# Wide attention layer of a twelve-layer kernel: where GpSimd computes its roots and sine products, and how the last output projection is portioned

## The reference

```python
# layer 10: 16 query heads of 128, 4 key/value heads, 2048 context rows + 128 own rows, batch of 2
q = rms_norm((x @ wq).reshape(B, L, 16, 128), q_norm_w)
k = rms_norm((x @ wk).reshape(B, L, 4, 128), k_norm_w)
v = (x @ wv).reshape(B, L, 4, 128)
k_ctx = rms_norm((h_ctx_kv @ wk_ctx).reshape(B, T, 4, 128), k_norm_w)
v_ctx = (h_ctx_kv @ wv_ctx).reshape(B, T, 4, 128)
q = q * cos + rotate_half(q) * sin
k = k * cos + rotate_half(k) * sin
...
scores = jnp.einsum('blhd,bmhd->bhlm', q, k_full) * scale + mask     # causal on the own rows
out = jnp.einsum('bhlm,bmhd->blhd', softmax(scores), v_full)
x = x + out.reshape(B, L, 16 * 128) @ wo
...
# layer 12: weights and activations rounded to float8 (e4m3) before each product
x = x + qdot(gelu(qdot(h, w_gating[0])) * qdot(h, w_gating[1]), w_linear)
```

## Time and profile before

| what | value |
|---|---|
| three timed runs | 1133.62, 1134.43 (median), 1134.64 us |
| the profiled execution, its own time | 1135.64 us |
| its span on the core | 1133.7 us |
| mean granted clock of TensorE | 0.975 |
| front of the wide layer, TensorE's first projection to its first score | 621.55 to 648.07 us |
| loop with 32 units | 648.07 to 1063.9 us |

### The profile page before, as it was taken

The page is one execution under the profiler, slowest core; times in us unless marked ns, Lnnn a source line. Parts: engine busy times, 40 slices in busy tenths (PEclk is TensorE's granted clock), DMA queues, the critical chain, the costliest instruction groups (busy, mean ns, idle before and its releaser), DMA issues.

```text
span 1133.7 us, 23178 instructions
## 1 busy us (share of the span) xinstructions
PE 1037.2 (91%) x9488; PEld 846.4 (75%) x9488; DVE 698.7 (62%) x1333; ACT 504.3 (44%) x871; POOL 234.0 (21%) x356
## 2 busy tenths in 40 slices
PE   6989999989999879999987989999999999999785
PEld 3755778866666545776775778999999999989664
DVE  3755243257777358888744776776666566677366
ACT  3242221126666437888855634433423223322374
POOL 5601048302122000000010511210010233331120
PEclk9998999998999979999999999999999999999897
DMA  9611346545663516000141000131111221100000
GB/s 387 274 74 63 137 159 222 195 120 141 175 172 100 173 39 235 22 3 2 38 150 38 1 1 20 38 113 38 38 57 38 60 63 57 57 20 10 0 2 10
DMA packets 37156, 100.37 MB, mean 89 GB/s; under 512 B 4032, under 2 KB 12608, under 8 KB 35392
## 3 DMA queue, kind: packets, MB, share of 16 engines
q1 hardware_dynamic: 33152, 87.35, 23.5%
q0 software_dynamic: 2752, 9.44, 2.5%
q10 hardware_dynamic: 1152, 2.16, 0.5%
HBM read 83.73 MB, written 15.20 MB: 87 GB/s over the span
## 4 chain that ended last, share of the span: by engine, by line
PE 71%; DVE 16%; issue 4%; POOL 4%; ACT 4%; DMA 1%; DVEq 0%; SPq 0%; ACTq 0%; POOLq 0%
PE ps L2192 9%; PE ps L390 8%; PE ps L2149 6%; PE ps L1372 6%; PE ps L1723 5%; PE ps L446 3%; PE ps L1714 3%; PE ps L383 3%; PE ps L2047 3%; PE ps L1520 3%; PE ps L2036 2%; DVE prob L2343 2%; PE ps L1058 2%; PE ps L1050 2%; DVE st L1649 2%
## 5 line engine op out<-in xcount | busy, mean ns | idle before, releaser
L2192 PE MATMUL ps<-vv,prob 128*128 128x129 f32 x1024 | 128.2, 278 | 2.6 <-DVE xn L2379 2.6
L2192 PEld LDWEIGHTS ps<-vv,prob 128*128 128x128 f32 x1024 | 121.7, 194 | 3.3 <-ACT prob L2298 3.0
L1649 DVE TENSOR_REDUCE st<-ps 128x1 f32<-128x512 f32 x128 | 83.4, 687 | 26.6 <-PE ps L1520 21.2
L2331 DVE TENSOR_REDUCE probT<-ps 128x128 f32<-128x1024 f32 x64 | 82.5, 1288 | 19.8 <-PE ps L2149 12.9
L2298 ACT ACTIVATE prob<-prob 128x1024 f32<-128x1024 f32 x64 | 71.1, 1111 | 27.4 <-DVE prob L2343 27.4
L390 PE MATMUL ps<-xT,big 128*128 128x256 f32 x352 | 79.8, 381 | 0.8 <-ACT xT L673 0.7
L2271 ACT COPY w<-ps 128x128 f32<-128x128 f32 x32 | 8.5, 265 | 161.7 <-PE ps L2158 161.7
L2343 DVE TENSOR_TENSOR prob<-ps,probT 128x1024 f32<-128x1024 f32 x64 | 79.6, 1286 | 1.1
L1596 ACT ACTIVATE prob<-ps 128x1024 f32<-128x1024 f32 x64 | 65.7, 1029 | 29.3 <-PE ps L1531 27.9
L152 POOL TENSOR_SCALAR small<-small 128x4 f32<-128x4 f32 (+1 forms) x44 | 13.0, 296 | 304.4 <-DVE small L2086 154.1
L390 PEld LDWEIGHTS ps<-xT,big 128*128 128x128 f32 x352 | 66.2, 190 | 11.3 <-ACT xT L673 0.9
(11 more groups left out here) (461 smaller groups left out, 2266.9 us busy)
## 6 DMA issues: line engine op xcount, KB each, us to landing
big<-blocks_in SPq DMA_DIRECT2D x22, 768.0 KB, 4.5
big<-ctxT_in SPq DMA_DIRECT2D x24, 512.0 KB, 4.1
key_parts<-w POOLq DMA_DIRECT2D x16, 384.0 KB, 5.3
kt<-key_parts SPq DMA_DIRECT2D x32, 192.0 KB, 3.3
vv<-ctx_in SPq DMA_DIRECT2D x2, 2176.0 KB, 23.9
vv<-early_values SPq DMA_DIRECT2D x4, 1088.0 KB, 12.8
kt<-ctxT_in SPq DMA_DIRECT2D x2, 2048.0 KB, 11.6
kt<-key_parts SPq DMA_DIRECT2D x32, 128.0 KB, 3.3
```

The source lines that it names most:

```text
L1649: dve.tensor_reduce(self.mx[:, u % 2, n:n + 1], k.ps[:, n % 2, :], AX.X, ALU.max).then_inc(s("reduced"), 1)
L2192: last = pe.matmul(k.ps[:, 7, 0:DH + 1], self.prob(u)[:, ch * P:ch * P + P], v, start=(ch == 0), stop=(ch == MC))
L2331: dve.tensor_reduce(self.largest[:, h * P:(h + 1) * P], bank.rearrange("p (c t) -> p t c", t=P), AX.X, ALU.max).then_inc(s("c3_max"), 1)
```

## The change

Three edits and one swap.

1. **Loop.** In steps 18 to 26 GpSimd's list was: add, subtract, root of the step's key group, load. It is now: add, root, subtract, load. (`weights_gpsimd` is cut into `weights_raised` and `weights_rounded`.)
2. **Front.** For q0 to q3 of batch 0 the product with the sines leaves VectorE's list; GpSimd makes it into another buffer (`sines`, `by_sine`). One semaphore, `w_own_made`, now counts roots and sine products in GpSimd's order (`SINES`, `SCALES`). The memsets `ones` come later. On ScalarE, `scale_heads` of q3 now precedes `square` of key group 4.
3. **End.** The output projection's heads in steps 28 to 32 were 4, 4, 3, 2, 1 and are now 3, 3, 3, 4, 1.

```diff
-    LAST_HEADS = {28: range(0, 4), 29: range(4, 8), 30: range(8, 11), 31: range(11, 13), 32: range(13, 14)}
+    LAST_HEADS = {28: range(0, 3), 29: range(3, 6), 30: range(6, 9), 31: range(9, 13), 32: range(13, 14)}
...
         o.step(dve.tensor_tensor(t3, h3, bc(self.table[:, first], 1, 4), ALU.mult))
-        o.step(dve.tensor_tensor(h3, h3, bc(self.table[:, first + 1], 1, 4), ALU.mult))
+        if b == 0 and n:
+            dve.wait_ge(s("w_own_made"), self.SINES[n])
+            h4 = self.by_sine(n).rearrange("p h (a d) -> p h a d", a=2)
+        else:
+            o.step(dve.tensor_tensor(h3, h3, bc(self.table[:, first + 1], 1, 4), ALU.mult))
...
+    def sines(self, pool, n):
+        k, s = self.k, self.k.s
+        pool.wait_ge(s("w_heads"), self.MADE.index(self.ROPED[n]) + 1)
+        if n >= 3:
+            pool.wait_ge(s("w_rope"), n - 1)
+        pool.tensor_tensor(self.by_sine(n), self.heads[0][n].rearrange("p (h d) -> p h d", h=4), bc(self.table[:, 1], 1, 4),
+                           ALU.mult).then_inc(s("w_own_made"), 1)
...
         self.copy_turned(act, 0, 2, 2)
+        self.scale_heads(act, 0, 4)
         self.square(act, 4, 3)
-        self.scale_heads(act, 0, 4)
...
         self.own_scales(pool, o, 0)
+        self.sines(pool, 1)
+        self.sines(pool, 2)
+        self.query_scales(pool, o, 0, 1)
+        self.sines(pool, 3)
+        self.query_scales(pool, o, 0, 2)
+        self.sines(pool, 4)
+        self.query_scales(pool, o, 0, 3)
         self.ones(pool, o)
-        for n in (1, 2, 3):
-            self.query_scales(pool, o, 0, n)
...
             if u >= self.EIGHT_AT:
-                eight.weights_gpsimd(pool, o, dram, u - self.EIGHT_AT)
+                eight.weights_raised(pool, o, u - self.EIGHT_AT)
             self.scales(pool, o, g)
             if u >= self.EIGHT_AT:
-                eight.weights_load(pool, dram, u - self.EIGHT_AT + 2)
+                eight.weights_rounded(pool, dram, u - self.EIGHT_AT)
```

More of the change, by code:

```diff
@@ L1861 @@
     EIGHT_AT = 18
-    LAST_HEADS = {28: range(0, 4), 29: range(4, 8), 30: range(8, 11), 31: range(11, 13), 32: range(13, 14)}
+    LAST_HEADS = {28: range(0, 3), 29: range(3, 6), 30: range(6, 9), 31: range(9, 13), 32: range(13, 14)}
     FIRST_VALUES = (0, 4, 1, 5, 2, 3)
     KEY_BANKS = (6, 7, 4, 5, 3)
+    SINES = (0, 2, 3, 5, 7)
+    SCALES = ((1, 4, 6, 8, 9), (10, 11, 12, 13, 14))
     def __init__(self, k):
@@ L1981, in rope @@
             o.step(last)
-            dve.wait_ge(s("w_own_rs"), 5 * b + 1)
+            dve.wait_ge(s("w_own_made"), self.SCALES[b][0])
             last = dve.tensor_tensor(t3, t3, bc(self.rs_k[b], 2, DH), ALU.mult)
@@ L1988, in scale_heads @@
         act.wait_ge(k.s("w_rope"), 5 * b + n + 1)
-        act.wait_ge(k.s("w_own_rs"), 5 * b + n + 1)
+        act.wait_ge(k.s("w_own_made"), self.SCALES[b][n])
         for h in range(4):
@@ L2019, in ones, with by_sine @@
         o.step(pool.memset(self.vs[:, :, :, DH:DH + 1], 1.0))
+    def sines(self, pool, n):
[5 more added lines that the diff above has]
+                           ALU.mult).then_inc(s("w_own_made"), 1)
+    def by_sine(self, n):
+        return self.heads[1][n].rearrange("p (h d) -> p h d", h=4)
     def own_scales(self, pool, o, b):
@@ L2023, in own_scales @@
         pool.wait_ge(s("w_own_ssq"), 5 * b + 1)
-        rsqrt_pool(k, pool, o, self.rs_k[b], self.ssq_k, 1.0 / DH, 1e-6, 4).then_inc(s("w_own_rs"), 1)
+        rsqrt_pool(k, pool, o, self.rs_k[b], self.ssq_k, 1.0 / DH, 1e-6, 4).then_inc(s("w_own_made"), 1)
     def query_scales(self, pool, o, b, n):
@@ L2412, in gpsimd @@
             if u >= self.EIGHT_AT:
-                eight.weights_gpsimd(pool, o, dram, u - self.EIGHT_AT)
+                eight.weights_raised(pool, o, u - self.EIGHT_AT)
             self.scales(pool, o, g)
             if u >= self.EIGHT_AT:
-                eight.weights_load(pool, dram, u - self.EIGHT_AT + 2)
+                eight.weights_rounded(pool, dram, u - self.EIGHT_AT)
         for i in range(self.GROUPS - F - self.EIGHT_AT, eight.PIECES):
-            eight.weights_gpsimd(pool, o, dram, i)
-            eight.weights_load(pool, dram, i + 2)
+            eight.weights_raised(pool, o, i)
+            eight.weights_rounded(pool, dram, i)
 class Differential:
@@ L2612, in weights_load, with weights_raised, weights_rounded @@
         pool.dma_start(self.raw[i % 2], dram["w8"][:, 512 * i:512 * i + 512]).then_inc(s(f"e8_in{i % 2}"), 16)
-    def weights_gpsimd(self, pool, o, dram, i):
-        s = self.k.s
+    def weights_raised(self, pool, o, i):
+        raw, tmp = self.raw[i % 2], self.tmp[i % 2]
+        pool.wait_ge(self.k.s("e8_power"), i + 1)
+        o.step(pool.tensor_tensor(raw, raw, tmp, ALU.add))
+    def weights_rounded(self, pool, dram, i):
         raw, tmp = self.raw[i % 2], self.tmp[i % 2]
         to = self.w_up[:, 512 * i:512 * i + 512] if i < 8 else self.w_down[:, 512 * i - 4096:512 * i - 3584]
-        pool.wait_ge(s("e8_power"), i + 1)
-        o.step(pool.tensor_tensor(raw, raw, tmp, ALU.add))
-        pool.tensor_tensor(to, raw, tmp, ALU.subtract).then_inc(s("e8_w"), 1)
+        pool.tensor_tensor(to, raw, tmp, ALU.subtract).then_inc(self.k.s("e8_w"), 1)
+        self.weights_load(pool, dram, i + 2)
     TURNED, GATE, UP, MADE = (4, 1), (5, 7, 2, 4), (6, 0, 3, 1), (5, 2)
```

2 lines of the change are left out of this document (1 added, 1 removed).

## The result

| | before | changed |
|---|---|---|
| median of the timed runs | 1134.54 us (4 runs, 1133.62 to 1138.63) | 1125.00 us (4 runs, 1121.01 to 1126.51) |
| ratio changed to before, 95% interval | | 0.9904 [0.9877, 0.9931] |
| the profiled execution, its own time | 1135.64 us | 1126.51 us |
| its span, granted clock | 1133.7 us, 0.975 | 1124.6 us, 0.976 |
| unit 0's shift to unit 31's shift | 396.62 us | 389.87 us |

The change made the kernel 1.0% faster. Forecast were 1126.3 us and a gain of 8.1 us, which is a ratio of 0.9929 and lies inside the interval; the profiled executions are 9.13 us apart. The ratio is that of the means, 1124.38 to 1135.33 us; times the median of 1134.43 that the prediction went by it gives 1123.5 us, under the range's lower end of 1123.8. One execution carries much of that: the kernel before took 1138.63 us in its fourth, which the prediction hadn't seen.

A forecast was written before the change was run, and what follows sets the result against it. TensorE, busy 91% of the span, was taken to bound the kernel, so gains come where it waits. Loop 6.8, front -0.4 and end 1.7 sum to 8.1 us, giving 1126.3 us; range 1123.8 to 1128.8 us.

The forecast's parts named there:

- the range's lower end of 1123.8: Whole kernel: low end of the forecast range, set to take in the front without holds (1124.0 us, 17%).
- nine times 0.75: Loop, steps 18 to 26: each step returns from 12.91 to 12.16 us, 6.8 us gained.
- half the gain: Loop rival: root ends later than computed or subtract delays the key scaling; 1129.7 us, 9%.
- no change: Loop rival: the subtract holds the key scaling (L2100) in full; 1133.1 us, 2%.
- the cover: Loop: root comes 0.1 us ahead of need; each 0.1 us later costs at most 0.9 us over nine steps.
- the 0.1 us added for GpSimd's roots: Front: GpSimd's roots of key groups 0 to 3 stand behind the sine products, adding 0.1 us.
- the forecast's upper bound, four whole instructions of 1.27 us: Front: if every hold is a full 1.27 us, the loss is 2.2 us.
- left the clock at 1.00: End: a 1.44 us wait at 646 kept the clock, so the last unit's 1.73 us wait might too.
- - 0.4: Front: 3.2 us held against 2.9 removed, plus roots; TensorE's first scores start 0.4 us later.
- the clock falls all the same: End rival: TensorE's clock still falls after the 1.73 us wait; 1128.0 us, 25%.
- The forecast's 1.7 us: End: clock stays at 2.4 GHz behind the shorter wait, last unit's 18 matmuls end 1.7 us sooner; bounds 0 and 1.8.
- the last of the sum: Whole kernel: 8.1 us off the profiled 1135.64 gives 1127.5, less 1.2 for the median, 1126.3 us.

The follow-up runs named there:

- half subtract ahead of the root: Changed kernel with the first 256 of the subtract's 512 columns put ahead of GpSimd's root again; one execution, 1128.14 us.
- kernel with the cosines from PSUM: Changed kernel with the cosine products of q0 to q3 reading the projections' PSUM banks instead of SBUF copies; 1127.33 us, ratio 0.9910.
- front's part alone: Kernel before with only the front's edit (sines on GpSimd, later squares of group 4); 1135.79 us, ratio 0.9986.
- old heads: Changed kernel with the old heads of the last out projection, so loop's and front's parts only; 1131.69 us, ratio 0.9959.
- loop's part alone: Kernel before with only the root moved between GpSimd's add and subtract; 1128.75 us, ratio 0.9921.
- spare matmuls: Changed kernel with unread matmuls, three heads ahead of the last unit's product and four behind the last out projection; 1124.01 us, ratio 0.9884.
- the same with the PSUM cosines: Changed kernel with unread matmuls in both waits and the cosine products of q0 to q3 read from PSUM; 1124.59 us, ratio 0.9885.

## Why the prediction was wrong, and what of it was right

**Loop: right, also in its size.** 6.75 us forecast (nine times 0.75), 6.75 measured between units 0 and 31, and 389.8 to 389.9 in each kernel that has the edit and the full subtract behind the root. The key scaling was not held by the subtract beside it (0.68 us): the rivals "half the gain" and "no change" are out. One sentence was too cautious: the cover was called 0.1 us thin and each later tenth priced. The half subtract ahead of the root shows 0.42 us more behind it. The load's issue came at 905.47, 0.46 us later than in the earlier trace rows, not "the same moment": the whole step is 0.21 us later (maxima at 902.88 against 902.67), and the issue waits 0.30 us for the subtract's end. Nothing needed it earlier.

**Front: right in its holds, incomplete in what follows from them.** Forecast were holds of 0.96, 0.60, 0.83 and 0.83 us; they were 0.95, 0.61, 0.76 and 0.75. TensorE started 0.17 us later, not 0.4: the last two holds were 0.15 us shorter together, and the 0.1 us added for GpSimd's roots didn't come. The kernel with the cosines from PSUM shows that what is held are the reads of SBUF. The Trainium skill (SBUF — State Buffer, section "Who interferes with whom") has the second of two such instructions blocked completely until the first has finished. The trace agrees: the three held cosine products end 0.54 to 0.55 us behind the end of their sine product (for instance 634.85 behind 634.30), the held addition 0.28 us behind it. So a hold is what is left of the first instruction when the second comes, and the forecast's upper bound, four whole instructions of 1.27 us, would need both to start at once.

What the forecast lacked is TensorE's clock at this place. It read from one trace that a wait of 1.44 us "left the clock at 1.00"; in three other traces the same wait, with 0.46 us behind it, was followed by a fallen clock. The front's part shortened that wait, so it probably gained more over many executions than its 0.14 us cost: its sign in the sum, - 0.4, is open.

**End: the last unit as forecast, the rest not.** With a wait of 1.73 us the 18 matmuls took 2.25 us in all six traces that have it: the rival "the clock falls all the same" didn't come. The forecast's 1.7 us is 1.64 in the pair of traces. But the premise was not a fixed one. After 2.59 to 2.60 us the clock fell in three traces (before, front's part alone, old heads) and stayed in one (loop's part alone). The line that the forecast drew between waits of 1.44 and 2.19 us, one trace for each side, isn't there: clocks fell behind 1.44 and 0.46, and stayed behind 1.73 and once behind 2.59.

**The step that failed** is the last of the sum: "Against the profiled execution's own 1135.64 us that gives 1127.5", less 1.2 for the median. It carries every other fall of the clock over from one execution of before, so the term for all clock falls but the last unit's was put at nothing. They are not the same from execution to execution, nor from kernel to kernel: over all executions the gain is 10.9 us where the sum had 8.1, and 3.3 of it go with the higher mean clock. The changed kernel's profiled execution, 1126.51 us, is 1.0 under the forecast 1127.5: 0.86 of it is regained behind unit 31 beside the last unit's 1.64 (2.50 - 1.64), and 0.23 in the front. Its median lies another 1.5 us below, not 1.2, and the fourth execution of before did the rest: these last two lie within the scatter of single executions. Over all executions the end's part is worth 1.5 us (alone, against before on the same chip), 1.1 (on the loop's part) and 5.5 (on loop and front) by mean times, the last two between different chips, where the sum had 1.7 once and for all. The range's lower end of 1123.8 was drawn from the front's holds alone and had no term for a mean clock above that of before.

**Open.** Why loop and front with the old heads run at a mean clock of 0.971 and the loop alone at 0.974 isn't settled; no run separates chance from cause there, and the traces show falls ahead of the wide layer that differ by chance. How the 3.3 us divide between the end of the front, the stretch behind unit 31 and chance is open too. That the falls behind the wide layer decide the rest is shown for the stretch of 1050 to 1104 us by the spare matmuls (clock 1.00, 75.2 us to the end instead of 77.5), but their worth in the median, 0.003, is within the two intervals.

The lowest ratios are those of the changed kernel with spare matmuls, 0.9884, and of the same with the PSUM cosines, 0.9885; the latter shorten the front by 1.1 us in the traces, though the medians don't show it.

## What to carry to other kernels

Where an engine's list has a short result that somebody waits for and a long one that nobody does, put the long one behind; its worth is the waiter's wait less the slack behind the waiter (here 1.17 - 0.42 = 0.75 us a step), and it can be read from one trace to a few hundredths. Moving an elementwise product from VectorE to GpSimd bought VectorE nothing here, while its own instructions read both inputs from SBUF: 2.9 us removed and 3.07 held. Price a clock fall as a chance and not as a fixed cost, take the chance from several traces of the place, and compare traces stage by stage before taking a difference of 2 us between executions for the change.

## What the runs showed of the hardware

- The granted clock fell after a wait of 2.59 or 2.60 us ahead of the last unit in three traces of four (18 matmuls in 3.88 or 3.89 us instead of 2.25). With a wait of 1.73 us in the same place it stayed in six of six, and with waits filled to 0.25 and 0.49 us it stayed at 1.00 over 1050 to 1104 us.
- At the end of the front it fell behind waits of 1.44 and 0.46 us in three traces of five, and in none of eight with shorter waits there.
- The mean clock of single executions of one and the same kernel goes from 0.969 to 0.978, and its time with it, 1131.7 to 1140.3 us for the kernel before. Ahead of the wide layer alone the same instructions take 618.6 to 624.1 us.
- A VectorE product with one input in PSUM (0.69 us) was not held by a GpSimd product of 512 columns beside it; one with both inputs in SBUF grew to 1.30 to 1.45. GpSimd's own took 1.27 us beside VectorE's and 1.45 where it had to get in.
